# Seven products over the whole depth of each aggregation in steps 2 to 4 of a gated graph network

## The chip, the cores and the metric

One core of one Trainium2 chip. The metric is the device time of one execution in microseconds; the median of three runs stands for the kernel. All arithmetic is fp32, done on TensorE as sums of products of a high part (fp32r) and a low part.

## The reference

```python
Af = A.astype(prop_state.dtype); AfT = Af.T
state = prop_state                      # 2048 x 256
for _ in range(5):
    s_in = state @ in_W.T + in_b
    s_out = state @ out_W.T + out_b
    a_in = Af @ s_in
    a_out = AfT @ s_out
    a = concatenate([a_in, a_out, state])
    r = sigmoid(a @ r_W.T + r_b)
    z = sigmoid(a @ z_W.T + z_b)
    joined = concatenate([a_in, a_out, r * state])
    h_hat = tanh(joined @ h_W.T + h_b)
    state = (1.0 - z) * state + z * h_hat
out = tanh(state @ o1_W.T + o1_b) @ o2_W.T + o2_b
x = layernorm(x + out)
```

The adjacency matrix A is 2048 x 2048, symmetric, of zeros and ones. The kernel uses the symmetry (and tests it on the way): it aggregates the state once, U = state^T A, and multiplies by weights folded beforehand.

## The kernel before

The 2048 nodes are four chunks of 512 columns (c = 0 to 3) and 16 blocks of 128 rows. The state is kept transposed (stateT) and as rows of nodes (rows, in a high and a low part). A is kept in SBUF as bytes (a8) and cast to fp32r tiles of two row blocks x 512 columns in a ring of four slots; PE multiplies them with the rows' high and low parts.

Step 0 aggregates chunk by chunk while A is loaded. Each of steps 1 to 4 has two sides: side 0 makes chunks 0 and 1, side 1 chunks 2 and 3. A side is one aggregation, followed by two gate chunks (L662 on PE, L950 and L985 on ScalarE, L1396 on VectorE).

The aggregation (L626 on PE, L1076 on ScalarE, L1508 on VectorE) works down the list ORDER (L68). For the first half of the depth (row blocks 0 to 7) it forms the four 512 x 128 results of a side from seven products P1 to P7 for eight, in the manner of Strassen and Winograd: each product has two ring tiles of 4 matmuls. The right factors are sums of blocks of A: P1, P2 and P4 use plain bytes, P6, P7 and P3 byte sums (sums) that GpSimd made beforehand (sum_blocks, L527) and that ScalarE casts with an offset, P5 the sum of two byte blocks that VectorE forms in its cast (L1186). The left factors are rows and differences of row blocks: T1 to T4 (t_add, L1251) with high and low parts (row_high, row_low). The second half of the depth has eight ordinary items of 8 matmuls. The mixes V, U3, W5, C12, C21, C22 (L1194) combine the banks after that; copy_p1 brings P1 from its bank for V.

A cast of item n waits until item n - 4 has been used (RING = 4). ScalarE makes 20 casts of a side, VectorE 2. All engines run their instructions in order; ScalarE and VectorE are ordered by hand in the functions named. The first four ScalarE casts of a side are made in the second gate chunk of the side ahead (gate_chunk_two, L985).

A gate chunk has six gates s (two halves of R, Z, H); each is an own part (6 matmuls on the state or on r*state) and a fold part (6 matmuls on the aggregate u_c), 72 matmuls. They use banks 4 to 6 in turn: gate s may start once gate s - 3's bank was read by VectorE (gate_read).

The new state goes back to row form by a transpose of 32 x 32 squares on VectorE (turn_state) and a DMA that moves the squares: turn_store and turn_load (L371) through DRAM for chunks 0 to 2, turn_move (L361 on SP's queue, L909 on ScalarE's) for chunk 3. VectorE also tests the symmetry of A in spare moments (test_symmetry, L1494).

## Time and profile before

| | |
|---|---|
| median of 3 runs | 661.55 us (661.32 to 661.77) |
| profiled execution | 660.54 us |
| its span, first to last instruction | 658.7 us |
| PE busy | 647.0 us, 98%, 2908 matmuls |
| VectorE busy | 481.5 us, 73% |
| ScalarE busy | 407.1 us, 62% |
| GpSimd busy | 51.1 us, 8% |
| granted TensorE clock, mean | 0.995 |

The span holds preparation and step 0 (to 146 us), steps 1 to 4 in eight sides of 60 us (146 to 626 us) and the output layers. Busy time of matmuls overlaps, since they are pipelined: one takes 0.39 us in the rows and the next one starts 0.23 us after it. The start-to-start distance is what counts for a stretch.

### The profile page before, as it was taken

How to read it: one execution, taken by the hardware profiler on the slowest of the kernel's cores; microseconds unless marked ns; L12 is line 12 of the kernel's file. 1: busy time of each engine (PE TensorE's matmuls, PEld its weight loads, DVE VectorE, ACT ScalarE, POOL GpSimd, SP SyncE). 2: the span in 40 equal slices, each digit the busy share in tenths (PEclk: the TensorE clock that was granted, in tenths of full speed). 3: DMA queues.
4: the chain of work that ended last, by engine and by line, in shares of the span. 5: the costliest groups of instructions: out<-in, count | busy, mean ns of one | idle time of the engine just before them, and what ended most of it. 6: DMA issues, size and time to landing. Idle time of an engine off the chain costs nothing.

```text
span 658.7 us, 8626 instructions
## 1 busy us (share of the span) xinstructions
PE 647.0 (98%) x2908; PEld 535.6 (81%) x2908; DVE 481.5 (73%) x782; ACT 407.1 (62%) x544; POOL 51.1 (8%) x49
## 2 busy tenths in 40 slices
PE   8999999999999999999999999999999999999994
PEld 7888888787888888888888888888888888888884
DVE  4986988897487569838784994677489658725887
ACT  2765554479457747855593788368368935763646
POOL 0191126100400000000000000000000000000002
PEclk9999999999999999999999999999999999999998
DMA  8998757222000221300013031000312200013003
GB/s 289 354 354 218 183 193 170 35 52 46 0 1 33 57 40 36 52 8 0 32 39 57 0 68 28 0 32 32 54 43 64 33 1 0 2 65 127 1 0 132
DMA packets 106803, 48.30 MB, mean 73 GB/s; under 512 B 88976, under 2 KB 95248, under 8 KB 106512
## 3 DMA queue, kind: packets, MB, share of 16 engines
q1 hardware_dynamic: 98256, 46.82, 25.9%
q10 hardware_dynamic: 8512, 1.05, 1.1%
q8 instruction: 17, 0.28, 0.2%
q14 instruction: 18, 0.15, 0.1%
HBM read 33.69 MB, written 11.53 MB: 69 GB/s over the span
## 4 chain that ended last, share of the span: by engine, by line
PE 95%; DVE 3%; issue 1%; ACT 0%; POOL 0%; DVEq 0%; POOLq 0%
PE bank L593 26%; PE bank L580 17%; PE bank L582 17%; PE bank L581 17%; PE bank L646 16%; PE bank L742 2%; PE bank L771 1%; DVE stats L1629 1%; DVE a L1622 0%; DVE deg_sum L1251 0%; DVE ring L1184 0%; PE bank L818 0%; ACT a L1168 0%; DVE work L1662 0%; DVE stateT L1228 0%
## 5 line engine op out<-in xcount | busy, mean ns | idle before, releaser
L593 PE MATMUL bank<-ring,rows 128*128 128x512 f32 x768 | 178.6, 389 | 0.0
L941 ACT ACTIVATE work<-work,bias 128x512 f32<-128x512 f32 x120 | 85.9, 722 | 149.1 <-DVE work L1349 148.5
L593 PEld LDWEIGHTS bank<-ring,rows 128*128 128x128 f32 x768 | 144.1, 188 | 30.1 <-issue 0.2
L1349 DVE SCALAR_TENSOR_TENSOR work<-degree,deg_w,bank 128x512 f32<-128x512 uint16 x120 | 88.6, 745 | 54.7 <-PE bank L582 53.9
L841 ACT ACTIVATE ring<-a 128x1024 fp32r<-128x1024 uint8 (+1 forms) x115 | 116.3, 1048 | 8.8 <-PE bank L593 6.6
L580 PE MATMUL bank<-u_c,fold 128*128 128x512 f32 x240 | 93.5, 390 | 0.0
L582 PE MATMUL bank<-u_c,fold 128*128 128x512 f32 x240 | 93.4, 389 | 0.0
L581 PE MATMUL bank<-u_c,fold 128*128 128x512 f32 x240 | 93.4, 389 | 0.0
L646 PE MATMUL bank<-ring,rows 128*128 128x512 f32 x256 | 65.1, 391 | 0.0
L580 PE MATMUL bank<-st_c,own 128*128 128x512 f32 x160 | 62.4, 390 | 0.3 <-DVE st_c L1184 0.3
L581 PE MATMUL bank<-st_c,own 128*128 128x512 f32 x160 | 62.3, 389 | 0.0
L582 PE MATMUL bank<-st_c,own 128*128 128x512 f32 x160 | 62.3, 389 | 0.0
L646 PEld LDWEIGHTS bank<-ring,rows 128*128 128x128 f32 x256 | 47.6, 188 | 11.2 <-issue 1.0
L871 ACT ACTIVATE ring<-sums,minus 128x1024 fp32r<-128x1024 uint8 x48 | 54.6, 1137 | 0.1
L582 PEld LDWEIGHTS bank<-u_c,fold 128*128 128x128 f32 x240 | 45.0, 188 | 9.4
L580 PEld LDWEIGHTS bank<-u_c,fold 128*128 128x128 f32 x240 | 45.1, 188 | 9.3
L581 PEld LDWEIGHTS bank<-u_c,fold 128*128 128x128 f32 x240 | 45.1, 188 | 9.3
L646 PE MATMUL bank<-ring,t_flat 128*128 128x512 f32 x192 | 46.7, 392 | 0.0
L1209 DVE TENSOR_TENSOR deg_sum<-bank,deg_sum 128x512 f32<-128x512 f32 x24 | 16.5, 689 | 39.5 <-PE bank L593 38.2
L1184 DVE TENSOR_TENSOR st_c<-stateT,st_c 128x512 fp32r<-128x512 f32 x40 | 27.0, 693 | 23.7 <-ACT st_c L841 23.6
L646 PEld LDWEIGHTS bank<-ring,t_flat 128*128 128x128 f32 x192 | 35.2, 188 | 8.9 <-ACT ring L841 0.8
L841 ACT ACTIVATE rs_c<-work 128x512 fp32r<-128x512 f32 x40 | 25.2, 630 | 25.3 <-DVE work L1359 24.5
(150 smaller groups left out, 921.5 us busy)
## 6 DMA issues: line engine op xcount, KB each, us to landing
stage<-in_adj_dram SPq DMA_DIRECT2D x15, 512.0 KB, 8.3
sums<-in_adj_dram SPq DMA_DIRECT2D x13, 512.0 KB, 5.9
turned_dram<-work SPq DMA_DIRECT2D x12, 512.0 KB, 2.6
rows<-turned_dram SPq DMA_DIRECT2D x192, 32.0 KB, 2.0
work<-in_x_dram SPq DMA_DIRECT2D x4, 512.0 KB, 10.6
x_dram<-work SPq DMA_DIRECT2D x4, 512.0 KB, 10.1
a<-x_dram SPq DMA_DIRECT2D x4, 512.0 KB, 5.3
a<-in_adj_dram SPq DMA_DIRECT2D x3, 512.0 KB, 11.0
```

The costliest lines, as they stand in the source:

```text
L580: nc.tensor.matmul(out_, wh, vh, start=first, stop=False)
L581: nc.tensor.matmul(out_, wh, vl, start=False, stop=False)
L582: return nc.tensor.matmul(out_, wl, vh, start=False, stop=last)
L593: m = nc.tensor.matmul(u_bank[2 * (c % 2) + d][:, :], rows[:, part, j, d * P:(d + 1) * P], tile[:, jj, :], start=(first and jj == 0 and pa ...
L646: last = nc.tensor.matmul(u_bank[BANK[kind]][:, :], product_rows(kind, part, 2 * p + jj), tile[:, jj, :], start=(kind in (P1, P5, P6, P4, ...
L742: return nc.tensor.matmul(b_[:, k * D:(k + 1) * D], lin_raw[:, m // DB, m % DB, k * P:(k + 1) * P], gate_T[g % 2][:, m, :], start=first, s ...
L841: nc.scalar.activation(out_, in_, ACT.Copy).then_inc(s, 1)
L871: nc.scalar.activation(ring[:, n % RING].rearrange("p j w -> p (j w)"), sums[:, 1 - side, m, h * 2 * CW:(h + 1) * 2 * CW], ACT.Identity, b ...
L941: nc.scalar.activation(gates[:, g, e, :], gates[:, g, e, :], ACT.Tanh if g == H else ACT.Sigmoid, bias=bias[:, g, e:e + 1]).then_inc(gate_ ...
L1184: nc.vector.tensor_tensor(out_, in_, hi_.bitcast(F32), ALU.subtract).then_inc(s, 1)
L1209: nc.vector.tensor_tensor(b, u_bank[bank_][:, :], a, ALU.add).then_inc(mixed, 1)
L1349: nc.vector.scalar_tensor_tensor(out=gates[:, g, e, :], in0=degree[:, c * CW:(c + 1) * CW], scalar=deg_w[:, g, e:e + 1], in1=g_bank[s % 3] ...
```

## The change

Steps 2 to 4 now use the seven products over the whole depth: 28 items of 4 matmuls a side. P1 to P7 have tiles p = 0 to 3; p = 2 and 3 belong to row blocks 8 to 15. Step 1 keeps the old list (HALF_ORDER, half_aggregate), with three changes: the state's split for the next side moves into gate_chunk_two, three own parts come ahead of the first gate chunk, and the symmetry tests are dealt out differently.

- PE: in steps 2 to 4 own parts 0 and 1 of the coming gate chunk run before item 8, own part 2 before item 18 (OWN_AT). P4 has a bank of its own (bank 7).
- The late left factors L11, L1 to L4, L21, L22 are made at side 0 by VectorE (l_add, row_low) and ScalarE (keep_l11, row_high). L2 lies in u_c, L3 and L4 in rs_c, both free during the aggregation; for side 1 they go through DRAM (keep_late, load_late).
- The byte sums of the late half: GpSimd makes them in step 1 (sum_blocks 2 and 3), they are stored in DRAM, and load_sums brings the set of each side back to the buffer sums.
- Casts of a side: 20 by ScalarE and 8 by VectorE (P5's four, P2's and P7's with p = 2 and 3).
- ScalarE copies P5's bank out (copy_p5) beside P1's. Five mixes for six.
- PE's and ScalarE's programs unroll step 1 and loop over steps 2 and 3, where they looped over steps 1 to 3.

The diff, cut to its core:

```diff
-    ORDER = [(P1, 0), (P1, 1), (P6, 0), (P6, 1), (P7, 0), (P7, 1), (P2, 0), (P2, 1), (P4, 0), (P4, 1), (P5, 0), (P5, 1),
-             (1, 4), (P3, 0), (0, 4), (P3, 1), (0, 5), (1, 5), (0, 6), (0, 7), (1, 6), (1, 7)]
+    ORDER = [(P1, 0), (P1, 1), (P6, 0), (P6, 1), (P7, 0), (P7, 1), (P4, 0), (P4, 1), (P1, 2), (P1, 3), (P5, 0), (P5, 1),
+             (P5, 2), (P5, 3), (P2, 0), (P2, 1), (P3, 0), (P3, 1), (P6, 2), (P6, 3), (P2, 2), (P2, 3), (P3, 2), (P3, 3),
+             (P7, 2), (P7, 3), (P4, 2), (P4, 3)]
     NI = len(ORDER)
-    BY_ACT = [n for n, (kind, _) in enumerate(ORDER) if kind != P5]
-    BY_VECTOR = [n for n in range(NI) if n not in BY_ACT]
-    V, U3, W5, C12, C21, C22 = range(1, 7)
+    HALF_ORDER = [(P1, 0), (P1, 1), (P6, 0), (P6, 1), (P7, 0), (P7, 1), (P2, 0), (P2, 1), (P4, 0), (P4, 1), (P5, 0), (P5, 1),
+                  (1, 4), (P3, 0), (0, 4), (P3, 1), (0, 5), (1, 5), (0, 6), (0, 7), (1, 6), (1, 7)]
+    HALF_NI = len(HALF_ORDER)
+    HALF_BY_ACT = [n for n, (kind, _) in enumerate(HALF_ORDER) if kind != P5]
+    HALF_BY_VECTOR = [n for n in range(HALF_NI) if n not in HALF_BY_ACT]
+    OWN_AT = {ORDER.index((P1, 2)): (0, 1), ORDER.index((P6, 2)): (2,)}
+    OWN_AHEAD = 3
+    BY_VECTOR = [n for n, (kind, p) in enumerate(ORDER) if kind == P5 or kind in (P2, P7) and p >= 2]
+    BY_ACT = [n for n in range(NI) if n not in BY_VECTOR]
+    V, C12, U3, C22, C21, W5 = "v", "c12", "u3", "c22", "c21", "w5"
+    MIXES = [V, C12, U3, C22, C21]
...
+            def keep_late(t):
+
+                sp.wait_ge(row_lo, row_count(t, (L2, 0)))
+                sp.dma_start(l2_dram, u_c[:, :, 0, :].bitcast(F32)).then_inc(l2_kept, 16)
+                sp.wait_ge(row_lo, row_count(t, (L4, 0)))
+                sp.dma_start(l34_dram, rs_c[:, :, :, :].bitcast(F32).rearrange("p s k w -> p (s k w)")).then_inc(l34_kept, 16)
+
+            def load_late(t):
+
+                sp.wait_ge(l2_kept, 16 * (t - 1))
+                sp.wait_ge(u_used, t * NC + 2)
+                sp.dma_start(u_c[:, :, 0, :].bitcast(F32), l2_dram).then_inc(late_back, 16)
+                sp.wait_ge(l34_kept, 16 * (t - 1))
+                sp.wait_ge(gate_done, t * S_GATE + 2 * GATE)
+                sp.dma_start(rs_c[:, :, :, :].bitcast(F32).rearrange("p s k w -> p (s k w)"), l34_dram).then_inc(late_back, 16)
+
+            def load_sums(t, side):
+
+                if (t, side) == (2, 0):
+                    sp.wait_ge(pair_used, used_at(1, 1, P3, 1))
+                else:
+                    sp.wait_ge(pair_used, used_at(t - 1 + side, 1 - side, P7, 3))
+                for h in range(2):
+                    sp.wait_ge(sums_kept[h], 32)
+                    sp.dma_start(sums[:, 1 - h].rearrange("p k w -> p (k w)"), sums_dram[side, h]).then_inc(sums_ready[h], 16)
+
+            def store_sums(side, h):
+
+                sp.wait_ge(sums_ready[side], 16 * (h + 1))
+                sp.dma_start(sums_dram[side, h], sums[:, 1 - side].rearrange("p k w -> p (k w)")).then_inc(sums_kept[side], 16)
...
+                if t > 1:
+                    keep_late(t)
+                    load_sums(t, 1)
                 turn_store(t, 0)
+                if t > 1:
+                    load_late(t)
                 turn_store(t, 1)
-                for k in range(2):
-                    turn_load(t, k)
+                turn_load(t, 0)
+                if t == 1:
+                    store_sums(0, 1)
+                turn_load(t, 1)
+                if t == 1:
+                    store_sums(1, 1)
+                load_sums(t + 1, 0)
...
+            pool.wait_ge(state_new, S_TWO + 2 * TWO)
+            pool.wait_ge(sums_kept[0], 16)
+            pool.wait_ge(pair_used, used_at(1, 0, P3, 1))
+            sum_blocks(2, range(6))
+            pool.wait_ge(sums_kept[1], 16)
+            pool.wait_ge(pair_used, used_at(1, 1, P3, 1))
+            sum_blocks(3, range(6))
...
+            BANK = {P1: u_bank[0], P2: u_bank[0], P5: u_bank[1], P3: u_bank[1], P6: u_bank[2], P7: u_bank[3], P4: t_bank}
+            NEEDS = {(P1, 0): ("b11", 0), (P5, 0): (T1, 0), (P6, 0): (T2, 0), (P7, 0): (T3, 0), (P2, 0): (1, 1), (P3, 0): (1, 1), (P4, 0): (T4, 0),
+                     (P1, 2): (L11, 0), (P5, 2): (L1, 0), (P6, 2): (L2, 0), (P7, 2): (L3, 0), (P2, 2): (L21, 0), (P3, 2): (L22, 0), (P4, 2): (L4, 0)}
+
+            def aggregate_pair(t, side):
+
+                pe.wait_ge(u_lo, t * S_TWO + side * 2 * TWO)
+                for n, (kind, p) in enumerate(ORDER):
+                    if n in OWN_AT:
+                        own_ahead(t, 2 * side, OWN_AT[n])
+                    tile = ring[:, n % RING]
+                    if n in BY_ACT:
+                        pe.wait_ge(pair_ready, groups(t, side, len(HALF_BY_ACT), len(BY_ACT), S_PAIR + BY_ACT.index(n) + 1))
+                    else:
+                        pe.wait_ge(std_cast, groups(t, side, len(HALF_BY_VECTOR), len(BY_VECTOR), BY_VECTOR.index(n) + 1))
+                    if side == 0 and p % 2 == 0:
+                        pe.wait_ge(row_lo, row_count(t, NEEDS[kind, p]))
+                    if side == 1 and (kind, p) == (P6, 2):
+                        pe.wait_ge(late_back, 32 * (t - 1))
+                    if (kind, p) == (P2, 0):
+                        pe.wait_ge(copied, groups(t, side, 1, 2, 1))
+                    if (kind, p) == (P3, 0):
+                        pe.wait_ge(copied, groups(t, side, 1, 2, 2))
+                    for jj in range(2):
+                        for part in (HI, LO):
+                            last = nc.tensor.matmul(BANK[kind][:, :], product_rows(kind, part, p, jj), tile[:, jj, :],
+                                                    start=(kind in (P1, P5, P6, P4, P7) and p == jj == 0 and part == HI),
+                                                    stop=(kind in (P1, P5, P6, P7, P4) and p == 3 and jj == 1 and part == LO),
+                                                    skip_group_check=kind in (P2, P3))
+                    last.then_inc(pair_used, 1)
+
+            def own_ahead(t, c, some):
+
+                pe.wait_ge(st_lo, t * S_TWO + (c + 1) * TWO)
+                for s in some:
+                    wait(pe, gate_read, t * S_GATE + c * GATE + s - 2)
+                    own_part(g_bank[s % 3], s // DB, s % DB, st_c)
 
             def gate_chunk(t, c, first=False, last_step=False):
                 if first:
@@ -670,8 +843,9 @@
...
-                    wait(pe, gate_read, t * S_GATE + c * GATE + s - 2)
-                    own_part(g_bank[s % 3], g, e, st_c)
+                    if first or c % 2 or s >= OWN_AHEAD:
+                        wait(pe, gate_read, t * S_GATE + c * GATE + s - 2)
+                        own_part(g_bank[s % 3], g, e, st_c)
...
+            def aggregate_pair(t, side):
+
+                for k in range(4, 8):
+                    cast(t, side, k)
+                if side == 0:
+                    keep_l11(t)
+                    row_high(t, L11, 0)
+                cast(t, side, 8)
+                if side == 0:
+                    turn_move(t - 1, range(2))
+                cast(t, side, 9)
+                if side == 0:
+                    turn_move(t - 1, range(2, 4))
+                    row_high(t, L1, 0)
+                    for h in range(2):
+                        row_high(t, 1, h)
+                copy_p1(t, side)
+                for k in range(10, 13):
+                    cast(t, side, k)
+                copy_p5(t, side)
+                cast(t, side, 13)
+                if side == 0:
+                    row_high(t, L2, 0)
+                cast(t, side, 14)
+                if side == 0:
+                    row_high(t, L21, 0)
+                cast(t, side, 15)
+                if side == 0:
+                    for k in (L22, L3, L4):
+                        row_high(t, k, 0)
+                cast(t, side, 16)
+                cast(t, side, 17)
+                split_u(t, 2 * side, 0, False)
+                cast(t, side, 18)
+                cast(t, side, 19)
+                split_u(t, 2 * side, 1, False)
 
             def step(t, first=False, last=False):
                 if first:
@@ -1111,7 +1368,7 @@
                             aggregate(t, c + 2)
...
+                if kind == P5:
+                    a, b = (a8[:, 2 * side + 1, (2 * h + k) * BC + 2 * (p % 2):(2 * h + k) * BC + 2 * (p % 2) + 2, :] for k in range(2))
+                    nc.vector.tensor_tensor(ring[:, n % RING], a, b, ALU.add).then_inc(std_cast, 1)
+                elif kind == P7:
+                    dve.wait_ge(sums_ready[h], sums_loads(t, side))
+                    nc.vector.tensor_scalar(ring[:, n % RING].rearrange("p j w -> p (j w)"), sums[:, 1 - h, 1, p % 2 * 2 * CW:(p % 2 + 1) * 2 * CW],
+                                            -1.0, 0.0, ALU.add, ALU.add).then_inc(std_cast, 1)
+                else:
+                    c, b = {P2: (2 * side, BC), P4: (2 * side + 1, BC)}[kind]
+                    b += 2 * BC * h + 2 * (p % 2)
...
+                b, a, product, last = {V: (low_, low_, u_bank[2], (P6, 3)), C12: (c12, low_, u_bank[1], (P3, 3)),
+                                       U3: (high_, low_, u_bank[3], (P7, 3)), C22: (c22, high_, p5, (P5, 3)),
+                                       C21: (c21, high_, t_bank, (P4, 3))}[what]
...
+            def l_add(t, k):
+
+                n = (t - 2) * 4 + ADDED_LATE.index(k)
+                raw = lambda q, d: rows[:, LO, q * BC:(q + 1) * BC, d * P:(d + 1) * P].bitcast(F32)
+                one, eleven, two = (s.rearrange("p (b d) -> p b d", b=BC) for s in spare)
+                if k == L1:
+                    dve.wait_ge(rows_loaded[2], 16 * NQ * NQ * t)
+                    dve.wait_ge(rs_ready, t * S_TWO)
+                else:
+                    dve.wait_ge(l_raw, n)
+                if k == L2:
+                    dve.wait_ge(rows_loaded[3], 16 * NQ * NQ * t)
+                    dve.wait_ge(state_new, t * S_TWO)
+                elif k == L4:
+                    dve.wait_ge(row_lo, row_count(t, (L1, 0)))
+                elif k == L3:
+                    dve.wait_ge(l11_kept, t - 1)
+                out_, a, b = {L1: (one, raw(2, 1), raw(2, 0)), L2: (two, raw(3, 1), one),
+                              L4: (one, raw(3, 0), two), L3: (eleven, two, eleven)}[k]
+                nc.vector.tensor_tensor(out_, a, b, ALU.subtract).then_inc(l_raw, 1)
...
-            ROWS_AT = {(2, 2): [("add", T1), ("add", T2)], (2, 3): [("low", ROWS[0]), ("low", ROWS[1]), ("add", T4), ("add", T3)],
-                       (3, 3): [("low", op) for op in ROWS[2:7]]}
+            ROWS_AT = {(2, 2): [("add", T1), ("add", T2)], (2, 3): [("low", ROWS[0]), ("low", ROWS[1])],
+                       (2, 4): [("add", T4), ("add", T3)],
+                       (3, 3): []}
...
+                if c == NC - 1 and not last or c == 1 and not first:
+                    for e in range(DB):
+                        split_state(*((t, 2) if c == 1 else (t + 1, 0)), e)
...
+            def aggregate_pair(t, side):
+
+                old = (t - 1, NC - 1) if side == 0 else (t, 1)
+                tested = iter(() if t == LAST else range(DB, 6 * DB) if side else range(DB))
+
+                def test():
+                    for n in tested:
+                        test_symmetry(t, n)
+                        break
+
+                update(*old)
+                if side == 0 or t < LAST:
+                    turn_state(*old)
+                if side == 0:
+                    l_add(t, L1)
+                    row_low(t, L11, 0)
+                cast(t, side, 0)
+                if side:
+                    test()
+                cast(t, side, 1)
+                if side == 0:
+                    row_low(t, L1, 0)
+                    for h in range(2):
+                        row_low(t, 1, h)
+                else:
+                    test()
+                    test()
+                cast(t, side, 2)
+                if side:
+                    test()
+                cast(t, side, 3)
+                for _ in range(4 if side else 2):
+                    test()
+                if side == 0:
+                    l_add(t, L2)
+                    l_add(t, L4)
+                    row_low(t, L2, 0)
+                    row_low(t, L21, 0)
+                    l_add(t, L3)
+                cast(t, side, 4)
+                test()
+                cast(t, side, 5)
+                test()
+                if side == 0:
+                    for k in (L22, L3, L4):
+                        row_low(t, k, 0)
+                mix(t, side, V)
+                cast(t, side, 6)
+                cast(t, side, 7)
+                mix(t, side, C12)
+                for d in range(DB):
+                    split_u(t, 2 * side, d)
+                mix(t, side, U3)
 
             def step(t, first=False, last=False):
                 if first:
```

## Rows read from the trace of the kernel before

**Rows 1.** The page: busy us (share) xinstructions; the ended-last chain by engine.
```profile
PE 647.0 (98%) x2908; PEld 535.6 (81%) x2908; DVE 481.5 (73%) x782; ACT 407.1 (62%) x544; POOL 51.1 (8%) x49
...
PE 95%; DVE 3%; issue 1%; ACT 0%; POOL 0%; DVEq 0%; POOLq 0%
```

**Rows 2.** Busy time by stretch, one side each: PE, PEld, DVE, ACT, POOL, clock, DMA.
```profile
146.40:206.40 60.00, 60.00 (x265) 49.22 (x264) 40.34 (x61) 38.05 (x50) 7.38 (x6) 1.00 0.12 24
...
326.40:386.40 60.00, 60.00 (x265) 49.35 (x265) 46.73 (x71) 39.76 (x53) 0.00 (x0) 1.00 0.18 39
386.40:446.40 60.00, 60.00 (x265) 49.38 (x264) 40.04 (x60) 37.79 (x50) 0.00 (x0) 1.00 0.11 22
```

**Rows 3.** The chain that ended last: start us, us, what.
```profile
446.62 11.01 PE bank L646 x48
...
463.06 10.88 PE bank L593 x48
...
506.58 11.01 PE bank L646 x48
```

**Rows 4.** ScalarE at the start of an aggregation (PE's first matmul 386.43).
```profile
387.41 0.72 ACT L941 ACTIVATE work<-work,bias 128x512 f32<-128x512 f32 x1 [0.64 <-DVE work L1349]
388.04 1.14 ACT L871 ACTIVATE ring<-sums,minus 128x1024 fp32r<-128x1024 uint8 x1
389.08 0.58 ACT L884 ACTIVATE deg_sum<-bank 128x512 f32<-128x512 f32 x1
389.56 1.14 ACT L871 ACTIVATE ring<-sums,minus 128x1024 fp32r<-128x1024 uint8 x1
390.60 2.94 ACT L841 ACTIVATE ring<-a 128x1024 fp32r<-128x1024 uint8 x3
```

**Rows 5.** VectorE at the start of the same aggregation.
```profile
386.63 0.75 DVE L1349 SCALAR_TENSOR_TENSOR work<-degree,deg_w,bank 128x512 f32<-128x512 uint16 x1 [0.61 <-PE bank L582]
...
388.17 0.69 DVE L1372 TENSOR_TENSOR work<-work,stateT 128x512 f32<-128x512 f32 x1 [0.19 <-ACT work L941]
388.78 1.29 DVE L1377 TENSOR_TENSOR work<-work 128x512 f32<-128x512 f32 x2
390.25 0.69 DVE L1209 TENSOR_TENSOR deg_sum<-bank,deg_sum 128x512 f32<-128x512 f32 x1 [0.19 <-PE bank L646]
...
392.06 1.30 DVE L1390 STREAM_TRANSPOSE work<-stateT 128x512 f32<-128x512 f32 x2
393.29 2.32 DVE L1192 TENSOR_TENSOR ring<-a 128x1024 fp32r<-128x1024 uint8 x2
```

**Rows 6.** VectorE by line: duration ns min/median/max, first and last start, form.
```profile
L1681 DVE CAST ones_r<-ones x1: 227/227/227, 1.7 to 1.7; 128x128 fp32r<-128x128 f32 x1
...
L1648 DVE TENSOR_SCALAR a<-a,mv,rstd x3: 382/408/413, 653.0 to 653.9; 128x256 f32<-128x256 f32 x3
...
L1192 DVE TENSOR_TENSOR ring<-a x16: 1180/1211/1225, 153.2 to 574.1; 128x1024 fp32r<-128x1024 uint8 x16
```

**Rows 7.** GpSimd's byte sums, and subtractions of VectorE beside one and alone.
```profile
99.94 1.04 POOL L539 TENSOR_TENSOR sums<-a,byte_two 128x512 uint32<-128x512 uint32 x1
...
105.99 1.30 POOL L539 TENSOR_TENSOR sums<-sums 128x512 uint32<-128x512 uint32 x1
...
100.17 1.97 DVE L1372 TENSOR_TENSOR work<-work,stateT 128x512 f32<-128x512 f32 x2
...
372.19 1.35 DVE L1372 TENSOR_TENSOR work<-work,stateT 128x512 f32<-128x512 f32 x2
```

**Rows 8.** SP's queue around the same aggregation, then DMA issues: KB each, us to landing.
```profile
381.75 7.70 SPq L383 DMA_DIRECT2D rows<-turned_dram  x16
393.39 7.94 SPq L367 DMA_DIRECT2D rows<-work  x12
...
rows<-turned_dram SPq DMA_DIRECT2D x192, 32.0 KB, 2.0
...
t_flat<-o_dram SPq DMA_DIRECT2D x1, 1024.0 KB, 4.7
```

**Rows 9.** PE's first matmul of chunk 3 in step 3, and VectorE's gate 2 there.
```profile
490.10 0.39 PE L580 MATMUL bank<-st_c,own 128*128 128x512 f32 x1
...
500.16 0.74 DVE L1349 SCALAR_TENSOR_TENSOR work<-degree,deg_w,bank 128x512 f32<-128x512 uint16 x1
```

309 lines of the change are left out of this document (223 added, 86 removed).

## The prediction

> **What bounds the kernel now.** I read the page first: PE is busy 98% of the span and 95% of the chain that ended last [rows 1]. A busy share can hide stalls, so the next view is the busy time by stretch over steps 1 to 4, cut at the starts of the aggregations: every side of 60.0 us shows PE busy for all of it, at a granted clock of 1.00, with VectorE busy for 40 to 47 us and ScalarE for 38 to 40 [rows 2]. Then the chain in order of time, for PE's pitch: 48 matmuls in 10.88 us are 0.2267 us each, and the next aggregation starts 60.0 us after the last [rows 3]. A side has 14 items of 4 matmuls, 8 of 8, and two gate chunks of 72, so 120 + 144 = 264 matmuls, which at 0.2267 are 59.8 us. So 0.1 to 0.2 us of a side is waiting. In this stretch the time is the number of matmuls.
>
> **What is removed.** A side of steps 2 to 4 now has 28 items of 4 matmuls, 112 for 120. 8 x 0.2267 = 1.81 us a side, and there are 6 sides: 48 matmuls, 10.88 us. The ones removed are ordinary ones, 128x512, one after the other, and I know of none that could already be hidden. Steps 0 and 1 keep their matmuls.
>
> **The new order on PE.** All times from here count from PE's first matmul of an aggregation. An item is 0.91 us, an own part (6 matmuls) 1.36. Items 0 to 7 run to 7.25, own parts 0 and 1 to 9.97, items 8 to 17 to 19.04, own part 2 to 20.40, items 18 to 27 to 29.5. Deadlines: P1's third tile 9.97, P5's four 11.8 to 14.5, P2's first 15.4, P3's first 17.2, P6's third 20.4, P2's third 22.2, P3's third 24.0, P7's third and fourth 25.8 and 26.8, P4's third 27.7. A tile can be cast only once the item four before it is done (ring of 4), so each cast has a window of 2.7 us.
>
> **ScalarE in that order.** From start to start a byte-sum cast takes 1.04 us, a plain one 0.95, a 512-wide copy about 0.5 [rows 4]. After the first aggregation item of step 2 or 3 it has 16 casts (8 of each kind, 15.9 us) and, on side 0, 14 small operations (7.3 us): 23.2 of 29.5 us. In queue order: its last two gates end at 1.7 as now [rows 4], casts 4 to 7 end at 5.6 (wanted by 6.35), the kept L11 and its high part 6.6, P1's third 7.6 and fourth 8.7 (wanted 10.9), L1 and row block 1 to 10.5. Copy_p1 waits for P1's last item, 11.8, and ends 12.3; PE wants it at 15.4. P2, P2, P3, copy_p5, P3 follow their ring slots and end at 17.2; L2's high part 17.7, P6's third 18.7 (wanted 20.4), L21, P6's fourth 20.3 (21.3), L22, L3, L4 to 21.8, P3's third 22.9 (24.0) and fourth 23.9 (24.9). The smallest slack is 0.7 us. Queued behind the new waits are only casts whose ring slot opens later. Cost: nothing; the cover is PE's own parts 0 and 1. Without them each want after item 7 comes 2.7 us earlier and copy_p1 starts at once, and P3's second tile (15.5 for 15.4) would be the first one late.
>
> **VectorE in that order.** A 512-wide operation takes 0.60 from start to start, the sum cast of P5 1.11 [rows 5]. Side 0 from the start of the aggregation: update 6, transposes 2, L adds 4, low parts 9, P5 casts 4, two tests, mixes 3, u splits 2, so 28 x 0.60 + 4.4 = 21.2, and four casts that it takes over from ScalarE (P2's and P7's late tiles). Gate 5 is read by 1.0, the update ends at 4.8, the transposes at 6.0 (mix V no longer stands between) [rows 5]. L1's add needs chunk 2's rows: their 16 loads are issued within 7.7 us from 4.7 before the start and land 2.0 later [rows 8], at 5.0, and with a later chunk 3 about 6.0. L11's low part 7.8, P5's first and second casts 10.0 (wanted 11.8, 12.7), three low parts 11.8, P5's third and fourth 14.0 (14.5). L2's add needs chunk 3's rows: 12 loads at 0.66 us behind the transposes, and the landing, 15.5 [rows 8]. L4's add 16.8, L2's low part behind ScalarE's high part 18.4 (wanted 20.4), L21 20.0, L3's add 20.6. Then P2's two casts, three low parts, V (2.4 us in all without the casts), P7's two, C12, two u splits, U3.
>
> **The price of the four casts** is what the trace doesn't show: one source in SBUF, uint8, 1024 wide. The full rate is 0.69 us for 512 and 1.21 for 1024 [rows 5, 6], a slope of 1.02 ns an element on 0.17. The copy ones_r (one source, 128 wide) took 0.227 [rows 6], where that line gives 0.30; at half the slope it would be 0.23, so a copy seems to go at double rate, and 1024 wide would be 0.69. The tensor_scalar of L1648 (256 wide) took 0.41 [rows 6], where the line gives 0.43: full rate. I take each cast by the row of its own kind: P2's at 0.6 a piece (pitch), P7's at 1.11. P2's then end at 21.8 (wanted 22.2, 23.1), V at 24.2, P7's at 25.4 and 26.5 (25.8, 26.8): just in time, cost 0. At 1.11 for all four, V ends at 25.2, P7's at 26.4 and 27.5: 0.6 + 0.2 = 0.8 us a side-0, three times. Side 1 has no row work and up to ten tests; its P7 casts wait for their slots at 23.1 and 24.0, and nothing is late.
>
> The Trainium skill (VectorE: DVE Perf Modes, section The perf-mode tier table) says that tensor_copy and tensor_scalar on fp32 in SBUF run at double rate. The ones_r row agrees; the tensor_scalar row, 0.41 us, does not. By the rule P7's casts would have 0.5 us more to spare each and the 0.8 could not come.
>
> **Gate chunks.** The first chunk of a side is now 12.2 us of PE for 16.3, since three own parts went ahead. VectorE's work in it stays except for the tests, which left it. R's chain: gates 0 and 1 are done at 1.4 and 2.7 after the fold's start, the low part of r*s at 7.2, PE wants it at 9.5. Side 1 of steps 1 to 3 also has four adds and two low parts. Adding the queue up with 0.60 and 0.66 and ScalarE's answers (0.8 a round trip) from the first gate at 1.6, gate 2 of chunk 3 is read at 24.2; PE wants that bank at 12.2 + 12.2 = 24.5. Now it is read 10.7 into chunk 3 against the same 12.2 [rows 9]. That leaves 0.3 where there was 1.5. The splits of the state moved from the aggregation to behind gate 3, where ScalarE and VectorE have room, three row operations having left the place. Gate 5 is then read at 1.2 instead of 1.0, inside the slacks above. I put 0.15 us on each of the three steps for these thin places, between 0 and 0.6: together 0.5.
>
> **Step 1.** GpSimd makes 2 x 6 more sums of 1.04 to 1.30 us [rows 7], 7.5 us each time. The first set starts when chunk 1's state is new, about 5.7 into side 1, beside P5's two sum casts, which now run 6.9 to 9.2 [rows 5]; PE wants them at 9.1 and 10.0. At 100.17 a subtraction of two SBUF operands beside GpSimd's sum (99.94 to 100.98) and its follower took 1.97 us instead of 1.35 [rows 7]: it stood until GpSimd's operation ended. If every cast waits for one sum, the second ends at about 11.3 and PE stands 1.3 us; if none does, 0. I take 0.7. The second set runs beside tests only. Its stores and loads of 768 KB (1 MB came back in 4.7 us [rows 8]) have 20 us before they are read.
>
> The Trainium skill (SBUF — State Buffer, section SBUF: two separate sides) calls this an exclusive lock that either engine holds for its whole instruction. The trace agrees by those 0.62 us. By a strict alternation the cost would be the 1.3.
>
> **The loads for late blocks.** keep_late and load_late put 0.5 and 1 MB out and back on SP's queue; the return starts with side 1 and lands at about 5.5 (4.7 for 1 MB [rows 8]), wanted at 20.4. load_sums waits for P7's last item, 27.7, and is read 20 us later. Behind it stand the stores of transposed state, whose data come later still. Cost 0.
>
> **The sum.** The profiled execution took 660.54 us, with a span of 658.7 and 1.8 around it; the runs' median is 661.55, 1.0 more. 660.54 - 10.88 + 0.7 + 0.5 = 650.9, and on the median 651.9.
>
> **Rivals.** (a) The late casts run at full rate: 0.8 x 3 = 2.4 more, 654.3. For it: the tensor_scalar row; against: the copy row. (b) The thin places give way together: 0.6 a side on six sides and 1.3 in step 1, 4.9 for my 1.2, 655.6. For it: five slacks of 0.5 us or less; against: PE's stalls give VectorE the time back. (c) Slower: chunk 3's rows come late to L2's add. ScalarE and VectorE are in order, so every later cast stands behind them, and PE stands from item 18 on. There are 2.0 us of slack behind the landing at 15.5; to eat 3.6 us a step it must land at 21 or later. If the twelve issues took twice their time (8 us more), 6 us a step would be lost: 18 - 10.9 = +7, 668.6. For it: SP's queue is longer now, with sums loads ahead; against: SP is idle when the transposes end, by its rows [rows 8]. (d) The change doesn't carry: waits for ring, copies and mixes I haven't seen eat about all, 661.5. Against: PE's order leaves each producer its window.
>
> **Chances.** Forecast 0.66 (650.0 to 653.3), (a) 0.17, (b) 0.08, (d) 0.04, (c) 0.05. The low end is the whole saving with step 1 free and some of the old 0.1 to 0.2 a side gone; the high end takes (a) and (b) in and leaves (c), (d) out: 650.0 to 655.8. Differences within 0.2% (1.3 us) a measurement of this kernel can't tell from none. Faster 0.91, same 0.04, slower 0.05.
>
> **What would show it.** Side length 58.1 to 58.4 in steps 2 to 4, 60.0 in step 1 but for 0.7 in its second side; 2860 matmuls; waits in the aggregations named for VectorE's ring casts (a), for DVE's gate reads in chunk 3 (b), for DMA rows (c). P7's cast at 1.2 and P2's at 0.7 decide the disputed price. It is wrong if a side is 59 or more.

## The result

The changed kernel takes 657.31 us (median of 6 runs, 656.97 to 657.93), the kernel before 661.72 in the same comparison (6 runs, 661.32 to 662.87). The ratio is 0.9932, with a 95% interval of 0.9919 to 0.9944: 4.4 us less, where the forecast was 9.7 less. The profiled execution took 657.65 us with a span of 655.9.

The matmuls went as counted. The page of the changed kernel, its busy line:

```profile
PE 638.1 (97%) x2860; PEld 525.3 (80%) x2860; DVE 524.4 (80%) x833; ACT 418.2 (64%) x562; POOL 68.1 (10%) x61
```

2860 is 48 fewer than in [rows 1], so the 10.9 us are gone from the sum of the work. VectorE has 43 us more to do, in a time that is shorter. The busy time by stretch of the changed kernel, cut at the starts of the aggregations from step 1 on (columns as in [rows 2]):

```profile
147.00:208.60 61.60, 60.54 (x265) 49.09 (x264) 46.68 (x68) 38.05 (x51) 8.35 (x6) 1.00 0.18 49
208.60:270.50 61.90, 60.61 (x265) 49.20 (x265) 45.11 (x64) 38.22 (x50) 15.89 (x12) 1.00 0.31 88
270.50:328.80 58.30, 58.30 (x258) 47.88 (x257) 49.32 (x74) 42.58 (x58) 0.00 (x0) 1.00 0.28 83
328.80:387.40 58.60, 58.31 (x257) 47.88 (x256) 50.19 (x75) 38.73 (x51) 0.00 (x0) 1.00 0.31 88
387.40:446.30 58.90, 58.59 (x258) 47.87 (x257) 49.19 (x74) 42.48 (x58) 0.00 (x0) 1.00 0.28 83
446.30:505.20 58.90, 58.61 (x258) 47.84 (x257) 49.70 (x71) 38.81 (x51) 0.00 (x0) 1.00 0.35 97
505.20:563.30 58.10, 58.10 (x257) 47.93 (x256) 50.41 (x85) 42.03 (x57) 0.00 (x0) 1.00 0.26 74
```

Against [rows 2] two things are to be seen. The sides of steps 2 to 4 fell from 60.0 to between 58.1 and 58.9 us; 58.1 is what 256 matmuls take without a stall. The two sides of step 1, which kept their products, grew from 60.0 to 61.6 and 61.9. The clock is 1.00 in every row. The next view shows what PE and its weight load wait for in the whole span (us in total, times, longest). The kernel before has none for VectorE's gates (L1679, there L1349), and 0.2 us for the byte-sum casts (L1050, there L871):

```profile
PEld bank L701 <- DVE work L1679: 3.7, 5, 1.0
...
PEld bank L765 <- ACT ring L1050: 1.9, 2, 1.2
...
PE bank L701 <- DVE work L1679: 1.5, 4, 0.6
...
PEld bank L765 <- DVE ring L1452: 1.4, 1, 1.4
...
PEld bank L822 <- DVE ring L1452: 1.0, 4, 0.4
```

PEld's waits overlap PE's work, so the loss is better read from PE's own starts: where two neighbours start more than their pitch of 0.227 us apart, the excess is stall. After 100 us it adds up to 7.2 us in the changed kernel and 1.3 in the kernel before. It comes in five groups, told in four paragraphs.

**Chunk 3 of steps 1 to 3: 0.61, 0.56 and 0.56 us.** PE and VectorE of the changed kernel in step 3, two fences of the timeline (start us, us, instruction, idle time before it):

```profile
500.28 0.39 PE L703 MATMUL bank<-u_c,fold 128*128 128x512 f32 x1
500.96 0.50 PE L701 MATMUL bank<-u_c,fold 128*128 128x512 f32 x1 [0.29 <-DVE work L1679]
```

```profile
497.77 1.30 DVE L1723 STREAM_TRANSPOSE work<-stateT 128x512 f32<-128x512 f32 x2
498.99 0.65 DVE L1442 TENSOR_TENSOR rs_c<-work,rs_c 128x512 fp32r<-128x512 f32 x1
499.56 0.68 DVE L1692 TENSOR_TENSOR work<-work,stateT 128x512 f32<-128x512 f32 x1
500.16 0.74 DVE L1679 SCALAR_TENSOR_TENSOR work<-degree,deg_w,bank 128x512 f32<-128x512 uint16 x1
```

PE comes to the bank of gate 2 at 500.51 and gets it at 500.96, when VectorE's read (500.16 to 500.90) is over. That read starts at 500.16 as it does in [rows 9]; there it was early enough.

**Step 0 to step 1: 0.31, 1.01 and 0.60 us** at 142.7, 151.5 and 153.0. ScalarE, then VectorE of the changed kernel, then VectorE of the kernel before:

```profile
149.04 1.38 ACT L1158 ACTIVATE work<-work,bias 128x512 f32<-128x512 f32 x2 [1.86 <-DVE work L1679]
150.33 1.13 ACT L1050 ACTIVATE ring<-sums,minus 128x1024 fp32r<-128x1024 uint8 x1
```

```profile
144.05 1.89 DVE L1442 TENSOR_TENSOR rows<-rows 128x512 fp32r<-128x512 f32 x3
145.86 1.29 DVE L1442 TENSOR_TENSOR t_flat<-deg_sum,t_flat 128x512 fp32r<-128x512 f32 x2
147.06 1.29 DVE L1442 TENSOR_TENSOR st_c<-stateT,st_c 128x512 fp32r<-128x512 f32 x2
148.27 1.40 DVE L1679 SCALAR_TENSOR_TENSOR work<-degree,deg_w,bank 128x512 f32<-128x512 uint16 x2
```

```profile
144.78 1.28 DVE L1184 TENSOR_TENSOR t_flat<-deg_sum,t_flat 128x512 fp32r<-128x512 f32 x2
145.99 1.40 DVE L1349 SCALAR_TENSOR_TENSOR work<-degree,deg_w,bank 128x512 f32<-128x512 uint16 x2
```

How full VectorE was over the end of step 0 in the kernel before, the last 22.8 us, with chunk 3 from 130.1 on in them (columns as in [rows 2]):

```profile
123.60:146.40 22.80, 22.54 (x100) 18.32 (x99) 22.53 (x37) 15.77 (x24) 0.00 (x0) 1.00 0.13 34
```

The two splits of the state (147.06) stand ahead of the last gates now: the change put them into the last gate chunk of step 0 too. In chunk 2 it moved the adds of T4 and T3 behind the splits of the state and of u, also in step 0. The gates are read 1.3 us behind the start of the aggregation (146.99), where they were read 0.4 ahead of it (145.99 for 146.40); ScalarE idles 1.86 us for them, and its next ring cast, queued behind, makes PE wait at 151.5.

**Step 1, side 1: 1.23 us** at 219.85. VectorE, GpSimd and PE of the changed kernel:

```profile
215.50 4.29 DVE L1452 TENSOR_TENSOR ring<-a 128x1024 fp32r<-128x1024 uint8 x2
```

```profile
215.44 1.04 POOL L647 TENSOR_TENSOR sums<-a,byte_two 128x512 uint32<-128x512 uint32 x1
216.56 2.15 POOL L647 TENSOR_TENSOR sums<-sums,a 128x512 uint32<-128x512 uint32 x1
218.79 2.15 POOL L647 TENSOR_TENSOR sums<-sums 128x512 uint32<-128x512 uint32 x1
```

```profile
219.85 0.73 PE L765 MATMUL bank<-ring,rows 128*128 128x512 f32 x2 [0.95 <-DVE ring L1452]
```

Two casts of P5 that took 2.32 us alone [rows 5] take 4.29 beside GpSimd's sums (2.06 and 2.31), and two of the sums take 2.15 for 1.30 [rows 7]. Each cast ends 1.08 us after the GpSimd operation that was running when it began (216.48 and 218.71).

**Step 3, side 0: 0.68 us** at 401.6 and 403.0, and 0.22 at 460.9. **Step 4, chunk 2: 0.86 us** at 602.1, and 0.20 at 594, which the kernel before has too, at 598. VectorE of the changed kernel in both places:

```profile
394.26 0.69 DVE L1519 TENSOR_TENSOR work<-rows 128x512 f32<-128x512 f32 x1 [0.29 <-DMA rows<-turned_dram]
...
400.21 2.35 DVE L1452 TENSOR_TENSOR ring<-a 128x1024 fp32r<-128x1024 uint8 x2
...
600.05 1.29 DVE L1442 TENSOR_TENSOR rows<-stateT,rows 128x512 fp32r<-128x512 f32 x2 [1.28 <-ACT rows L1017]
...
601.33 0.73 DVE L1679 SCALAR_TENSOR_TENSOR work<-degree,deg_w,bank 128x512 f32<-128x512 uint16 x1
```

In step 3 P5's last two casts end at 402.56, 15.1 us after the start of the aggregation (387.43); PE wants the last at 14.5. In step 4 VectorE waits 1.28 us for ScalarE at the copy of the state for the output layers (final_split), with the read of gate 2 queued behind it, and PE stands from 601.36 to 602.11. The kernel before has the same order and the same wait of 1.28; there the read ended at 605.17 and PE wanted the bank at 606.28, here it ends at 602.06.

The groups sum to 1.73 + 1.92 + 1.23 + 0.90 + 1.06 = 6.8 us of the 7.2.

### The profile page after: what moved, and what is told of

It is laid out like the page before. It is cut to its first block and busy times, and to the rows that moved or that the text cites. A ratio compares the mean times of both kernels' runs of the same rounds, so it can differ in the third digit from the quotient of the medians.

```text
span 655.9 us, 8678 instructions
## 1 busy us (share of the span) xinstructions
PE 638.1 (97%) x2860; PEld 525.3 (80%) x2860; DVE 524.4 (80%) x833; ACT 418.2 (64%) x562; POOL 68.1 (10%) x61
## 3 DMA queue, kind: packets, MB, share of 16 engines
q10 hardware_dynamic: 8512, 1.05, 1.1%
## 5 line engine op out<-in xcount | busy, mean ns | idle before, releaser
L1679 DVE SCALAR_TENSOR_TENSOR work<-degree,deg_w,bank 128x512 f32<-128x512 uint16 x120 | 88.4, 744 | 28.1 <-PE bank L703 27.3
L1017 ACT ACTIVATE ring<-a 128x1024 fp32r<-128x1024 uint8 (+1 forms) x91 | 91.7, 1048 | 6.3 <-PE bank L822 3.1
L822 PE MATMUL bank<-ring,rows 128*128 128x512 f32 x384 | 90.8, 390 | 0.3 <-DVE ring L1452 0.3
L714 PE MATMUL bank<-ring,rows 128*128 128x512 f32 x384 | 88.6, 389 | 0.2 <-issue 0.2
L1050 ACT ACTIVATE ring<-sums,minus 128x1024 fp32r<-128x1024 uint8 x72 | 80.3, 1139 | 7.5 <-PE bank L822 6.5
L822 PEld LDWEIGHTS bank<-ring,rows 128*128 128x128 f32 x384 | 71.7, 188 | 16.5 <-DVE ring L1452 1.0
L714 PEld LDWEIGHTS bank<-ring,rows 128*128 128x128 f32 x384 | 72.0, 188 | 15.5 <-issue 0.6
L1017 ACT ACTIVATE rs_c<-work 128x512 fp32r<-128x512 f32 x46 | 28.6, 629 | 25.8 <-DVE work L1692 25.8
L687 POOL TENSOR_TENSOR ring<-stateT,ring 128x512 fp32r<-128x512 f32 x1 | 1.7, 1681 | 403.3 <-DVE rows L1442 403.3
L1452 DVE TENSOR_TENSOR ring<-a 128x1024 fp32r<-128x1024 uint8 x28 | 35.2, 1286 | 5.6 <-PE bank L822 5.6
L701 PEld LDWEIGHTS bank<-st_c,own 128*128 128x128 f32 x160 | 30.0, 188 | 6.8 <-DVE st_c L1442 0.3
```

The costliest lines, as they stand in the source:

```text
L701: nc.tensor.matmul(out_, wh, vh, start=first, stop=False)
L714: m = nc.tensor.matmul(u_bank[2 * (c % 2) + d][:, :], rows[:, part, j, d * P:(d + 1) * P], tile[:, jj, :], start=(first and jj == 0 and pa ...
L822: last = nc.tensor.matmul(BANK[kind][:, :], product_rows(kind, part, p, jj), tile[:, jj, :], start=(kind in (P1, P5, P6, P4, P7) and p == ...
L1017: nc.scalar.activation(out_, in_, ACT.Copy).then_inc(s, 1)
L1050: nc.scalar.activation(ring[:, n % RING].rearrange("p j w -> p (j w)"), sums[:, 1 - (side if half(t) else h), m, p % 2 * 2 * CW:(p % 2 + 1 ...
L1452: nc.vector.tensor_tensor(ring[:, n % RING], a, b, ALU.add).then_inc(std_cast, 1)
```

## The experiments

Each stall has a suspect: instructions that stand ahead, on the same engine, of the one PE waits for. Each run moves one of them and leaves the rest. By the first theory of each expectation the stall is a local matter of order and its price comes back when the order is mended; by the second the engine has no time left there, and the stall only moves. Differences between two changed kernels are of medians, against the 656.95 us of the changed kernel's second measurement; each ratio to the kernel before has its 95% interval. The interval of every single move that gains overlaps the changed kernel's own (0.9915 to 0.9948), and their medians fall by up to 0.7 us more than the stalls that go. So what one move is worth is read from the stalls in its trace; the medians settle only the four moves together and the two orders in chunk 3.

**The changed kernel again.**

> The changed kernel once more, on the chip of the three below. Both theories: 0.993 of the kernel before, and the same stalls on PE at the same places as in its first profile: 1.9 us around the start of step 1, 1.2 us in step 1's second aggregation, 0.6 us in chunk 3 of steps 1 to 3, 0.8 us in step 3's first aggregation and 0.9 us in step 4's chunk 2. A stall that doesn't come back belongs to that execution and not to the change.

Measured: 656.95 us, the kernel before 661.25 beside it, 0.9931 (0.9915 to 0.9948). Its stalls lie at the same instructions and differ by at most 0.06 us each, but for the first at 401, which is 0.11 more: their places belong to the program, not to one execution. The size of the one at 401 to 403 does vary. In the seven profiles with the cast order and chunk 3 as changed it is 0.50 to 0.93 us, 0.93 in final_alone, which does nothing there.

**The split of the state back in the aggregation of step 1.**

```diff
-                if not ending:
+                if not ending and not first:
                     for e in range(DB):
                         split_state(*((t, 2) if c == 1 else (t + 1, 0)), e)
...
                 for k in range(12, 16):
                     cast(t, side, k)
+                    if side == 0 and k % 2 == 1:
+                        split_state(t, 0, k // 2 - 6)
```

(ScalarE's half; VectorE's is moved likewise, between its tests.)

> The state's split for step 1's first side goes back from the last gate chunk of step 0 into the aggregation; all else as changed. Theory 1 (order): step 0's last chunk still had its five row operations when the two splits were added, so gates 4 and 5 were read late and everything behind them; PE's three stalls at 142.7, 151.5 and 153.0 (0.3 + 1.0 + 0.6 = 1.9 us) go and the first side of step 1 takes 60.1 us, not 61.65. Theory 2 (VectorE and ScalarE have no room left): the work comes back in the aggregation and casts are late there; less than half of the 1.9 us is gained and a new stall stands later in the side.

Measured: 655.75 us, 0.9919 (0.9902 to 0.9935), 1.2 less than the changed kernel. Step 1's first side is 60.5 us for 61.65. The stall at 153 is gone and that at 151.6 is down to 0.46; the one at 142 (0.31) stays. So the splits were 1.15 of the 1.92 us; the rest had another cause.

**GpSimd's third set behind P5's casts.**

```diff
             pool.wait_ge(pair_used, used_at(1, 0, P3, 1))
+            pool.wait_ge(std_cast, 4)
             sum_blocks(2, range(6))
```

> GpSimd's third set of byte sums (step 1, side 1) waits until VectorE's two casts of P5 there are done; all else as changed. Theory 1 (the two engines stop each other): the casts take 1.2 us each again instead of 4.3 us for both, PE's stall of 1.2 us at 219.9 goes. Theory 2 (the casts are long for another reason, such as the DMA traffic of that stretch): 4.3 us and the stall stay. If the stop works both ways, the symmetry tests behind stretch instead, without a stall.

Measured: 655.17 us, 0.991 (0.9893 to 0.9926), 1.8 less. VectorE and GpSimd of this kernel:

```profile
215.06 2.31 DVE L1453 TENSOR_TENSOR ring<-a 128x1024 fp32r<-128x1024 uint8 x2
```

```profile
217.90 1.04 POOL L647 TENSOR_TENSOR sums<-a,byte_one 128x512 uint32<-128x512 uint32 x1 [41.77 <-DVE ring L1453]
```

The casts take 2.31 us again, and the stall of 1.23 us is gone whole. The other 0.5 us of the difference has no stall of that place behind it. GpSimd's six sums, 3.5 us later, are late for nobody; they run beside the symmetry tests now, which take up to 1.67 us for 0.69 without making PE wait.

**Gate 2 of chunk 3 ahead of the transposes.**

```diff
                     final(0)
+                    early = c == NC - 1 and not last
+                    if early:
+                        gate(t, c, 2)
                     if not last:
                         turn_state(t, c - 1)
```

> In chunk 3 of steps 0 to 3 VectorE reads gate 2 ahead of the two transposes instead of behind them; all else as changed. Theory 1 (order): the stall of 0.6 us in chunk 3 of steps 1, 2 and 3, 1.7 us in all, goes and nothing takes its place. Theory 2 (VectorE is out of time in chunks 2 and 3): the low part of r*s or gates 3 to 5 come late in place of gate 2, or the transposed rows land later and stall the next aggregation; less than half is gained.

Measured: 658.59 us, 0.9963 (0.9949 to 0.9977): 1.6 us slower than the changed kernel. VectorE in step 3:

```profile
500.59 0.65 DVE L1442 TENSOR_TENSOR rs_c<-work,rs_c 128x512 fp32r<-128x512 f32 x1
...
502.54 0.69 DVE L1442 TENSOR_TENSOR rs_c<-work,rs_c 128x512 fp32r<-128x512 f32 x1 [0.70 <-ACT rs_c L1017]
```

The gate is in time, and now the second low part of r*s, whose wait for ScalarE the gate used to fill, is the late one: VectorE idles 0.70 us, and PE stalls 0.74, 0.59 and 0.59 at that tile where it stalled 0.61, 0.56 and 0.56 at the bank. New stalls of 0.40 to 0.48 follow at the start of each aggregation of steps 2 to 4, and the one at 151 grows from 1.05 to 1.62. The stall moved, as the second theory had it.

**As split_back, and the row adds of step 0 back in their old place.**

```diff
+                    at = ROWS_AT[c, n]
+                    if first and (c, n) == (2, 3):
+                        at = at + ROWS_AT[2, 4]
+                    elif first and (c, n) == (2, 4):
+                        return
```

> As split_back, and in step 0 alone T4's and T3's adds go back in front of the state's and u's splits, as the kernel before has them; all else as changed. Theory 1 (order): step 0's last chunk is again that of the kernel before, so what split_back left there (0.3 us at 142.5, 0.5 us at 151.6) goes too and the first side of step 1 takes 60.1 us; 1.9 us less than the changed kernel. Theory 2 (the remainder comes from the aggregation of step 1, not from step 0): the 0.5 us stays.

Measured: 655.61 us, the kernel before 661.46 beside it, 0.9907 (0.989 to 0.9923). Step 1's first side, by stretch:

```profile
146.30:206.20 59.90, 59.90 (x265) 49.09 (x264) 45.74 (x68) 38.58 (x51) 8.54 (x6) 1.00 0.19 51
```

The stalls at 142, 151 and 153 are all gone, and the side is as long as in [rows 2]. In their place stands 0.54 us at 130.6, which the kernel before has too (0.53 at 129.8). Of the 1.92 us some 1.4 come back; the first theory had expected all of it.

**Gate 2 of chunk 3 between the two transposes.**

```diff
-                        turn_state(t, c - 1)
+                        turn_state(t, c - 1, range(1) if early else range(2))
+                    if early:
+                        gate(t, c, 2)
                     rs_low(t, c, 0)
                     rs(t, c, 1)
+                    if early:
+                        turn_state(t, c - 1, range(1, 2))
```

> In chunk 3 of steps 0 to 3 VectorE reads gate 2 between the two transposes, and the second transpose stands between the second r*s and its low part, so that each answer of ScalarE is still covered by other work; all else as changed. Theory 1 (gate_early failed because VectorE then idled for 0.7 us before the low part): the 0.6 us in chunk 3 of steps 1 to 3 goes. Theory 2 (no time left): the transposed rows are stored 1.8 us later, land when ScalarE already waits for them, and the next aggregation's P1 tile is late by 0.5 us or more: the stall changes its place and the time stays within 0.5 us.

Measured: 661.48 us (10 runs), 0.9998 (0.9989 to 1.0008). The whole gain of the change is lost by one half transpose that comes later. The two sides of step 2, then ScalarE in its first aggregation:

```profile
270.10:330.20 60.10, 58.99 (x258) 47.63 (x257) 49.74 (x75) 42.91 (x58) 0.00 (x0) 1.00 0.29 85
330.20:388.30 58.10, 58.10 (x258) 47.91 (x257) 49.66 (x74) 38.19 (x51) 0.00 (x0) 1.00 0.30 86
```

```profile
278.20 0.63 ACT L1079 ACTIVATE work<-rows 128x512 f32<-128x512 f32 x1 [1.35 <-DMA rows<-turned_dram]
```

The side with chunk 3's gate in it is 58.1 us, without a stall. But the transposed state leaves for DRAM and comes back later, ScalarE waits 1.35 us for it in the next aggregation (1.53 in step 3) and VectorE 0.90 (1.09), P5's casts queued behind shift, and PE stalls 1.3 to 1.5 us at the last two of them. The second theory named the place; it put the loss within 0.5 us, and it was 4.5. The chunk-3 stall can't be ordered away like this: the three jobs of VectorE there (gate, low part, transposes) are each wanted at once, and the transposes dearest of all.

**Two late places: final_split one gate later in step 4, and P5's casts ahead of row block 1's low parts.**

```diff
-    FINAL_AT = {(2, 1): 0, (2, 2): 1, (3, 2): 2}
+    FINAL_AT = {(2, 2): 0, (2, 3): 1, (3, 2): 2}
...
                 gate(t, c, 3)
+                final(3)
...
                     row_low(t, L1, 0)
-                    for h in range(2):
-                        row_low(t, 1, h)
...
                 cast(t, side, 3)
+                if side == 0:
+                    for h in range(2):
+                        row_low(t, 1, h)
```

> Two places that lie apart, each with its own stall on PE: (i) in step 4's chunk 2 the final state's two splits come one gate later, so that gate 2 is read first; (ii) in side 0 of steps 2 to 4 the low parts of row block 1 come behind P5's last two casts instead of ahead. Theory 1 (order): the 0.9 us at 601.8 goes, and the 0.6 us at 401.3 with the 0.1 us behind it; 1.5 us in all. Theory 2 (time): (i) comes back as a late low part of r*s 1.4 us later, (ii) as a late P2 tile.

Measured: 654.94 us, 0.9897 (0.9881 to 0.9914). The stalls at 602 (0.86) and at 401 to 403 (0.68) are gone; 0.57 us of new ones stand at 285 to 287 in step 2. ScalarE, then VectorE there:

```profile
278.24 2.07 ACTq L1117 DMA_DIRECT2D rows<-work  x1
```

```profile
282.72 0.69 DVE L1442 TENSOR_TENSOR rows<-work,rows 128x512 fp32r<-128x512 f32 x1 [1.49 <-ACT rows L1017]
```

One issue of turn_move on ScalarE's queue took 2.07 us, where it takes 0.87 in the changed kernel. ScalarE's next cast and the high part of L1 come late, VectorE waits 1.49 us for that part, and P5's casts queued behind it are late. The profiled execution is also the slowest of this kernel's four (656.39).

**All four moves together** (step0_as_before, sums_later, late_two).

> step0_as_before, sums_later and both moves of late_two together; chunk 3 as changed. Theory 1: the gains are of separate places and add up, 1.9 + 1.2 + 1.5 = 4.6 us less than the changed kernel, about 0.986 of the kernel before; PE keeps the 0.6 us in chunk 3 of steps 1 to 3. Theory 2: one gain uncovers the next late operation and they add up to less than 3 us.

Measured: 652.17 us (651.48 to 652.52), the kernel before 661.46, 0.986 (0.9843 to 0.9876). It beats both kernels, by 9.3 and about 5 us: the gains add up to the 4.6 us of the first theory. Its excess over the pitch after 100 us is 2.9 us for 7.2.

**The copy of the state alone.** Only the FINAL_AT and final(3) part of late_two's edit.

> Only step 4's share of the last run but one: the copy of the state (final_split) stands one gate later in chunk 2, ahead of nothing that PE needs soon; the row operations stand as in the changed kernel. Theory 1 (each stall in the trace is one instruction too many ahead of a read that PE waits for, and the stalls add): the stall at 602 (0.86 us) is gone, those at 401 to 403 (0.68 us) stay, the sides of step 2 stay at 58.2; 0.9 us less than the changed kernel, so 656.1 to 656.5. Theory 2 (VectorE's work in that chunk just fits and the stall moves to the next gate): 657.0, with a new stall in chunk 2 or 3 of step 4.

Measured: 655.75 us, the kernel before 661.3, 0.9914 (0.9898 to 0.9931). The stall at 602 is gone, the others stay (the one at 401 to 403 with 0.93), no new one comes. The time is 0.35 us below the range of the first theory, which the stalls don't explain.

**P5's casts first, alone.** Only the other part.

> Only the other share: VectorE makes the last two casts of P5 before the two low parts of row block 1. Theory 1 (P5's casts were late because these two row operations stood ahead of them, and the low parts have time): the stalls at 401 to 403 (0.68 us) are gone, step 2 stays at 58.2 a side; 0.7 less, 656.3 to 656.7. Theory 2 (what was gained there is given back by what reads the low parts): step 3 gains 0.7, step 2's first side gets 0.5 (as its trace in the joint run had at 285 to 287), together 0.2 less, 656.8 to 657.2, not to be told from the changed kernel.

Measured: 655.73 us, 0.9913 (0.9897 to 0.993). Of the 0.68 us at 401 to 403, 0.11 stay; step 2 stays at 58.2 a side. Up to step 4 this is the program of late_two, so the new stalls of late_two in step 2 don't come from this order alone. The time is again 0.6 us below the range of the first theory. VectorE of this kernel in step 3:

```profile
393.93 0.69 DVE L1519 TENSOR_TENSOR work<-rows 128x512 f32<-128x512 f32 x1 [0.56 <-DMA rows<-turned_dram]
...
398.67 2.35 DVE L1452 TENSOR_TENSOR ring<-a 128x1024 fp32r<-128x1024 uint8 x2
400.94 1.29 DVE L1442 TENSOR_TENSOR rows<-rows 128x512 fp32r<-128x512 f32 x2
```

The rows landed 0.27 us later here than in the changed kernel's trace (a wait of 0.56 for 0.29), and the casts were still early enough. With the old order and a like wait (0.55 in final_alone) the stall was 0.93.

**The four moves with and without the cast order.** three_moves leaves the cast order as it was, four_again is the kernel with four moves once more.

> The four moves without the cast order: the splits of step 0 and 1 as in the kernel before, GpSimd's third set later, the copy of the state one gate later in step 4. If stalls add, this saves 1.5 (splits) + 1.5 (sums) + 0.9 (copy) = 3.9 us on the changed kernel, 653.0 to 653.6, and stands 0.2 to 1.0 behind the kernel with four moves. If the cast order was worth nothing there either, both are equal within 0.3 us.

> The kernel with four moves once more, beside the one with three: 652.2 again (651.7 to 652.7), and against three_moves what the cast order is worth: 0.7 less by the stalls at 401 to 403, 0.2 less if step 2 gives 0.5 of it back, 0 if it depends on the execution.

Measured: 652.72 us (652.33 to 653.72), 0.9873 (0.9857 to 0.989), and 652.18 (651.49 to 652.7), 0.9858 (0.9842 to 0.9875). The kernel with three is 0.3 us below the range expected, the one with four repeats within 0.01 us. What the cast order adds to the other three, 0.5 us, lies inside the intervals. The first side of step 3 in four_again:

```profile
384.00:442.70 58.70, 58.61 (x258) 47.83 (x258) 49.16 (x74) 42.44 (x58) 0.00 (x0) 1.00 0.29 84
```

This side has 0.47 us of stall at P5's casts in spite of the better order; three_moves has 0.50. ScalarE of four_again waits 1.38 us there for the transposed rows, which it waits 0.46 for in four_moves, the same program:

```profile
391.57 0.63 ACT L1080 ACTIVATE work<-rows 128x512 f32<-128x512 f32 x1 [1.38 <-DMA rows<-turned_dram]
```

The difference begins at one DMA issue on SP's queue, the second of the 16 loads of these rows. It took 1.89 us in four_again, 1.33 in four_moves and 1.32 in three_moves. So these two traces can't tell what the order is worth; casts_first beside final_alone can.

## Why the prediction was wrong

The direction and the mechanism were right: a matmul out of PE's queue is worth its pitch, 256 of them take the 58.1 us forecast, and the waits that come instead were named in part. The term that failed is the sum of the waits: I had put 1.2 us (0.7 in step 1 and 0.5 in the gate chunks) where 5.9 came. The largest part of them, 1.9 us from step 0 to step 1, I had put at nothing. 661.72 - 10.88 + 5.9 (stall after 100 us, 7.2 for 1.3) = 656.7, near the 657.3 measured; 0.6 us are not settled. In the profiled execution alone, step 0's first aggregation starts 0.9 us later and the end takes 1.1 longer behind the last matmul. From that matmul to VectorE's last operation both take the same to 0.1 us, so the 1.1 lie behind it. Of the signs that I named, "a side is 59 or more" came true in step 1 alone (61.6 and 61.9). Step by step:

- **Removed matmuls, 10.88 us:** right. So were ScalarE's queue (no wait of PE for it in steps 2 to 4 of the changed kernel) and the side lengths where nothing stalls, 58.1 and 58.2.
- **The price of the four casts:** the disputed price was settled the cheap way. The changed kernel, by line:

```profile
L1452 DVE TENSOR_TENSOR ring<-a 128x1024 fp32r<-128x1024 uint8 x28 | 35.2, 1286 | 5.6 <-PE bank L822 5.6
L1460 DVE CAST ring<-a 128x1024 fp32r<-128x1024 uint8 x12 | 8.0, 690 | 8.6 <-PE bank L822 8.6
L1455 DVE TENSOR_SCALAR ring<-sums 128x1024 fp32r<-128x1024 uint8 x12 | 8.0, 689 | 1.3 <-PE bank L822 1.3
```

P2's cast takes 0.690 us as taken, and P7's 0.689, where I had 1.21 (1.11 from start to start) from the row of L1648 [rows 6]. That row is 256 wide, and its two scalars are columns in SBUF: it was not the nearest row to a 1024-wide cast with a constant. The rule of the Trainium skill (VectorE: DVE Perf Modes, The perf-mode tier table), double rate for a tensor_scalar on fp32 in SBUF, held against it, here with bytes as the source: 0.689 us where the tensor_tensor of that size takes 1.21. The row of L1648, which is fp32 in SBUF, stays slower than the rule has it; whether its column scalars are the reason no run shows. Rival (a) fell; the row cost no time in the sum.
- **Gate chunks, 0.15 us a step:** mis-sized; 0.58. "gate 2 of chunk 3 is read at 24.2; PE wants that bank at 12.2 + 12.2 = 24.5" set the start of the read against the wanted time. The read begins at 24.1 (500.16) but lasts 0.74, and PE gets the bank at 24.9. For the kernel before I had taken the end: "read 10.7 into chunk 3" is the 10.80 at which it ends by [rows 9], not the 10.06 at which it starts. A slack must be taken at the end of the instruction that frees the thing. With the end, my own numbers give 0.4 to 0.5 us a step.
- **"The splits of the state moved from the aggregation to behind gate 3, where ScalarE and VectorE have room, three row operations having left the place":** false for the passage from step 0 to 1, which keeps its five row operations (HALF_ROWS). VectorE was busy 22.53 of 22.80 us there in the kernel before (row above), a stretch that I hadn't read. 1.9 us instead of nothing; split_back and step0_as_before give some 1.4 of it back. I costed an edit by its place in steps 2 to 4 and didn't look at its first occurrence.
- **GpSimd beside P5's casts, 0.7 (0 to 1.3):** 1.23, the upper bound. The trace had an operation that stood until GpSimd's was over [rows 7], and I took the middle. It is what the exclusive lock of the Trainium skill (SBUF — State Buffer, SBUF: two separate sides) makes of it: the two engines alternate, so each of the two casts waits for one GpSimd operation, and each of the two that follow on GpSimd for one cast. The trace agrees by 4.29 for 2.32 and 2.15 for 1.30.
- **"P5's third and fourth 14.0 (14.5)":** the fourth ended at 14.5 in step 2 and 15.1 in step 3. L1's add starts 6.5 and 6.8 us after the start for my 6.0; in step 3 the rows landed late and cost 0.3 of it. Two low parts stood ahead that nobody wanted yet. 0.9 us with the 0.22 of 460.9, where the sum had nothing.
- **Step 4, chunk 2:** not looked at. final_split stood ahead of gate 2 as before, but the end of that read went from 1.1 us ahead of PE's want to 0.7 behind it: 0.86 us, final_alone shows it.
- **Rival (b), the thin places together, 655.6:** the nearest and by mechanism the right one. It had the 1.3 of GpSimd, and 0.6 on each of six sides where 0.6 came on three, 0.7 on one; but the two places that nobody had costed (1.9 and 0.86) make it too low as well. I gave it 0.08 with the reason that PE's stalls give VectorE the time back; no run tests that reason, and all five groups came.
- **Rival (c), rows late to L2's add:** its add starts 16.8 us after the start in step 2 for my 15.5, after a wait of 0.96 for DMA; of 2.0 us of slack 0.7 were left. gate_between shows what later landings cost, there at L1's add (8.1 for 6.5): the full gain gone.

The forecast, 651.9, is near what the kernel with four moves takes (652.2 in both comparisons), but that is in part luck: my 1.2 us of waits were 0.7 beside GpSimd and 0.5 in chunk 3, and that kernel has none beside GpSimd and 1.7 in chunk 3. The saving was there; the changed kernel paid for it in five places, of which four could be mended by order alone. Left are the 1.7 us of chunk 3, where two orders were tried and neither paid.
